# Linear attention one sequence per step instead of in pairs, and an LSTM scratch tile in PSUM

## The chip, the cores and the metric

The kernel is one program on one core of a Trainium2 chip. The metric is device time in microseconds (us) of one execution. TensorE (PE) does matmuls and transposes, VectorE (DVE), ScalarE (ACT) and GpSimd (POOL) do elementwise work, SyncE issues DMAs. Each has its own in-order queue; they meet through semaphores only.

## The reference, cut to what matters

Twelve layers run over 16 sequences of 128 tokens by 128 features. Each computes `x = layernorm(x + layer(x))`. The change touches two of them.

The first is an LSTM of 20 units over 128 tokens, whose states steer a Gaussian attention:

```python
g = xg_t + h @ W_hh.T
i, f, gg, o = jnp.split(g, 4, axis=-1)
c = jax.nn.sigmoid(f) * c + jax.nn.sigmoid(i) * jnp.tanh(gg)
h = jax.nn.sigmoid(o) * jnp.tanh(c)
```

The fourth is causal linear attention with 16 heads of 8 features, and a layernorm of its own:

```python
q = (jax.nn.elu(q) + 1.0 + FEAT_EPS) / jnp.sqrt(jnp.asarray(E, q.dtype))
k = jax.nn.elu(k) + 1.0 + FEAT_EPS
kv_cumsum = jnp.cumsum(jnp.einsum('blhe,blhf->blhef', k, v), axis=1)
num = jnp.einsum('blhe,blhef->blhf', q, kv_cumsum)
den = jnp.einsum('blhe,blhe->blh', q, jnp.cumsum(k, axis=1))[..., None] + FEAT_EPS
out = (num / den).reshape(B, L, D) @ Wout.T + bout
return (out - mu) / jnp.sqrt(var + LN_EPS) * gamma + beta
```

Both kernels compute it as scores k q^T, kept where the key is not later than the query and zero elsewhere, times V with a column of ones that yields the denominator.

## The kernel before, in words

All 16 sequences stay in SBUF (`x_all`); each stage (S_LSTM, S_X0, S_SIM, S_REG, S_LIN, S_X1, ...) reads and overwrites them. Each engine runs its own function of a stage, then the next stage's; `seq_done` counts finished sequences. Nothing is planned: the order is written out by hand, per engine.

The linear-attention stage, S_LIN, uses the general `att_*` functions with `kind == "linear"`. They work on pairs: sequence s of a pair (s = 0 or 1) has `arena[s]` and the four PSUM banks `ps[s]`. A hardware loop goes over seven of the eight pairs. For each pair:

- POOL copies x (line 471), widens the queries to four head slots (`widen`, line 451), and takes reciprocal square roots as powers (`rstd`, line 356).
- PE does the scores: four matmuls of 32 rows (four heads) by 512 columns in four banks (line 550); values, 16 matmuls of 32 output rows (line 572); four transposes (line 600); projections of the pair two further on (lines 525 to 538); the transpose of the head output (609) and the output projection (616, bias 338).
- DVE multiplies each 128x512 bank of scores by a triangle of zeros and ones (line 746), divides by the denominator (772 to 783), makes the feature map from Exp (714, 732 to 736), and does both layernorms (798, 362 to 379, 811, 371).
- ACT only copies out of PSUM (639, 655, 682, 690) and takes one Exp (660).

What precedes S_LIN is S_REG, of the same functions; what follows is S_X1 (lines 1809 on). S_FF1 (lines 1920 to 2042) and S_FF2 are written in another manner: a Python loop, fully unrolled, of one sequence per step, in which each engine works in one step on several sequences in different phases.

The LSTM is 128 steps, each a ring of PE (line 1504), ACT (1530, 1533), DVE (1547, 1549), ACT (1535, which writes the tanh of the cell, `tanh_c`, a tile of 20x16 in SBUF), DVE (1552, which reads it and writes the state). Bank `ps[0][0]` holds in this time only the means of four weight matrices, once, in step 25.

## Time and profile before

| | us |
|---|---|
| median of 3 runs (2166.25 to 2170.86) | 2168.05 |
| the profiled execution | 2166.34 |
| its span, first to last instruction | 2164.5 |
| busy in the span: PE | 1637.6 |
| DVE | 1280.6 |
| ACT | 917.1 |
| POOL | 539.3 |

The mean granted clock of PE was 0.847 of full speed. A line of the profile names the source line, engine and operation, then output and input tiles, and how often it came; busy time and mean duration follow, then the time for which the engine was idle just before, with what ended it. PE matmuls are pipelined: a matmul in fp32 is recorded as two instructions.

### The profile page before, as it was taken

To read this page: it belongs to the slowest core of one execution; us is meant where nothing else is said; L and a number is where in the kernel's file an instruction comes from. 1 tells how busy PE (TensorE), PEld (TensorE's weight loads), DVE (VectorE), ACT (ScalarE), POOL (GpSimd) and SP (SyncE) were. 2 spreads that over 40 slices of the span, in tenths; PEclk is the share of its full clock that TensorE was granted. 3 is DMA by queue.
4 is the path that set the end of the run, shared out by engine and by line. 5 is a ranking of instruction groups with operands and counts; after the bars stand their busy time and mean duration, and the time that the engine had idled before them with its cause. 6 is when DMAs were issued, how large, how long until landed. Compare 5 with 4: busy or idle time off the path is not lost.

```text
span 2164.5 us, 44201 instructions
## 1 busy us (share of the span) xinstructions
PE 1637.6 (76%) x14699; PEld 1045.7 (48%) x14699; DVE 1280.6 (59%) x3907; ACT 917.1 (42%) x2683; POOL 539.3 (25%) x902
## 2 busy tenths in 40 slices
PE   4555489767776556889777863389799999996997
PEld 3333355434443335545444532156467777773443
DVE  2333556556666775721675768766656666653776
ACT  3332334447651113443443444433355665662433
POOL 2321422211112223310122213312134434341110
PEclk6555599779996778899898985599999999997999
DMA  5000000000000000000002000000000000000000
GB/s 199 1 1 1 1 1 0 0 1 0 0 0 0 0 0 0 1 0 1 1 0 101 0 1 0 0 2 0 0 1 1 0 0 0 0 1 0 0 0 19
DMA packets 2933, 18.34 MB, mean 8 GB/s; under 512 B 1049, under 2 KB 1177, under 8 KB 1561
## 3 DMA queue, kind: packets, MB, share of 16 engines
q1 hardware_dynamic: 2842, 17.17, 2.1%
q8 instruction: 52, 0.85, 0.2%
q14 instruction: 39, 0.32, 0.0%
HBM read 16.06 MB, written 1.05 MB: 8 GB/s over the span
## 4 chain that ended last, share of the span: by engine, by line
PE 57%; issue 17%; DVE 9%; ACT 7%; POOL 4%; DVEq 4%; POOLq 1%; DMA 0%; ACTq 0%; SPq 0%
PE ps L2825 5%; PE ps L916 3%; PE ps L930 3%; PE ps L2390 3%; PE ps L2400 3%; PE ps L2414 3%; PE ps L2369 3%; PE ps L2376 3%; PE ps L985 2%; PE ps L2234 2%; PE ps L1504 2%; PE ps L338 2%; POOL arena L356 2%; PE ps L895 2%; PE ps L550 2%
## 5 line engine op out<-in xcount | busy, mean ns | idle before, releaser
L356 POOL TENSOR_TENSOR arena<-arena,C 128x1 f32<-128x1 f32 (+1 forms) x208 | 118.0, 570 | 640.7 <-DVE arena L367 328.7
L1075 DVE TENSOR_REDUCE arena<-ps 128x4 f32<-128x512 f32 x256 | 164.1, 685 | 89.6 <-PE ps L926 50.4
L2327 POOL TENSOR_TENSOR arena<-arena 128x512 f32<-128x512 f32 x128 | 132.7, 1042 | 233.6 <-DVE arena L2615 233.1
L451 POOL TENSOR_TENSOR arena<-arena,C 128x512 f32<-128x512 f32 x96 | 99.8, 1040 | 363.7 <-ACT arena L652 124.6
L1043 ACT ACTIVATE arena<-ps 128x512 f32<-128x512 f32 x256 | 132.2, 603 | 91.5 <-PE ps L942 91.5
L2825 PE MATMUL ps<-WA,arena 128*128 128x512 f32 x256 | 133.4, 603 | 0.4 <-ACT arena L2849 0.4
L1504 PE MATMUL ps<-hid,WA 128*20 128x16 f32 x1024 | 57.2, 196 | 95.5 <-DVE hid L1552 95.5
L2524 ACT ACTIVATE arena<-ps,arena 128x256 f32<-128x256 f32 x256 | 119.9, 477 | 11.8 <-issue 8.1
L2533 ACT COPY arena<-ps 128x512 f32<-128x512 f32 x128 | 69.1, 589 | 121.5 <-PE ps L2400 121.5
L2607 DVE TENSOR_REDUCE arena<-ps 128x2 f32<-128x512 f32 x128 | 82.5, 686 | 43.9 <-PE ps L2390 42.5
L550 PE MATMUL ps<-arena 32*128 32x512 f32 x256 | 54.4, 907 | 63.2 <-POOL arena L451 63.2
L1504 PEld LDWEIGHTS ps<-hid,WA 128*20 128x20 f32 x1024 | 43.6, 116 | 117.7 <-DVE hid L1552 117.2
L338 PE MATMUL ps<-bias,ones_b 128*128 128x128 bf16 (+1 forms) x336 | 98.8, 294 | 0.0
L930 PE MATMUL ps<-arena 32*128 32x512 f32 x512 | 76.8, 671 | 16.8 <-DVE arena L1075 16.7
L916 PE MATMUL ps<-arena 32*128 32x128 f32 x2048 | 77.1, 288 | 15.1 <-DVE arena L1101 11.2
L2857 ACT ACTIVATE arena<-ps 128x256 f32<-128x256 f32 x128 | 49.0, 383 | 91.7 <-PE ps L338 91.7
L916 PEld LDWEIGHTS ps<-arena 32*128 32x128 f32 x2048 | 66.6, 192 | 31.7 <-issue 19.9
L985 PE MATMUL ps<-arena 128*32 128x128 f32 x2048 | 77.8, 281 | 3.6 <-ACT arena L1043 2.7
L371 DVE TENSOR_SCALAR x_all<-arena 128x128 f32 (+1 forms) x160 | 65.9, 412 | 19.9 <-POOL arena L356 19.4
L1547 DVE SCALAR_TENSOR_TENSOR prod<-gates 20x32 f32<-20x32 f32 x128 | 23.0, 180 | 90.7 <-ACT gates L1530 90.7
L2400 PE MATMUL ps<-C,arena 128*128 128x128 f32 x512 | 70.8, 280 | 3.7 <-POOL arena L2327 3.7
L2390 PE MATMUL ps<-arena 64*128 64x256 f32 x512 | 72.6, 402 | 0.0
(444 smaller groups left out, 4110.5 us busy)
## 6 DMA issues: line engine op xcount, KB each, us to landing
WA<-w_late SPq DMA_DIRECT2D x1, 4228.0 KB, 12.9
WA<-w_early SPq DMA_DIRECT2D x1, 1600.0 KB
R<-rows SPq DMA_DIRECT2D x1, 1282.0 KB, 6.8
WB<-w_rest SPq DMA_DIRECT2D x1, 1152.0 KB, 11.2
xT_all<-x_T SPq DMA_DIRECT2D x1, 1024.0 KB, 6.6
x_all<-x_tok SPq DMA_DIRECT2D x1, 1024.0 KB, 13.7
arena<-mask SPq DMA_DIRECT2D x1, 1024.0 KB
ctxT_all<-ctx_T SPq DMA_DIRECT2D x1, 1024.0 KB
```

What stands on the lines that cost most here:

```text
L338: return nc.tensor.matmul(out_ap, ones_b[:, :], bias3[:, BIAS(name, of, width)], start=False, stop=stop, skip_group_check=True)
L356: nc.gpsimd.tensor_tensor(v_(s, cols, "rstd", 0, n), v_(s, cols, "mv", 1, 2 * n - 1)[:, ::2] if n > 1 else v_(s, cols, "mv", 1, 1), cst("m ...
L916: mm = nc.tensor.matmul(ps[z][t][:, 128 * j:128 * j + 128], v_(z, ATT, "P", WIDE_Q + 128 * j, 128)[rows(t), :], v_(z, ATT, "kT")[rows(t), ...
L930: nc.tensor.matmul(ps[s][t][:, :], v_(s, ATT, "kT")[rows(t), :], v_(s, ATT, "P", WIDE_Q, 512)[rows(t), :], start=True, stop=False, skip_gr ...
L985: mm = nc.tensor.matmul(ps[s][2][PAD * j:PAD * (j + 1), t * 128:(t + 1) * 128], va[:, 4 * t + j, :], v_(s, ATT, "PT", 128 * (4 * t + j), 128),
L1043: nc.scalar.activation(v_(s, ATT, "PT", 512 * t, 512), ps[s][t][:, :], ACT.Exp, scale=SCALE).then_inc(pT_sb, 1)
L1075: red = nc.vector.tensor_reduce(v_(z, ATT, "m", 4 * t, 4), heads(ps[z][t][:, :]), AXX, ALU.max)
L1504: mm = nc.tensor.matmul(bank(k // HALF, gt)[:, k % HALF, :], W_of(*weights("hh", gt)), h, start=False, stop=True, skip_group_check=True)
L2327: nc.gpsimd.tensor_tensor(p, p, v_(z, LAT, "rec", 4 * u + 2 * x, 2).unsqueeze(2).broadcast_to([128, 2, 256]), ALU.mult).then_inc(l_sub, 1)
L2390: mm = nc.tensor.matmul(score_bank(u, x)[:, 256 * j:256 * j + 256], v_(z, LAT, "qT", 128 * (2 * u + j), 128)[rows, :], kT[rows, 2 * u + j, :],
L2400: mm = nc.tensor.transpose(score_bank(u, x)[:, 128 * c:128 * c + 128], P_of(s, u, x)[:, 128 * c:128 * c + 128], ident)
L2825: nc.tensor.matmul(o, v_(s, MOE, "xT"), WA[:, W_LATE("experts", FF * e, FF)], start=True, stop=False, skip_group_check=True)
```

## The change

The S_LIN stage gets functions of its own in place of the `att_*` ones: an unrolled pipeline of single sequences. A sequence has one working area, in the arena that its number's parity picks, and all sequences share eight banks: four for scores (`ps[1]`), one for the projections, one for transposes of x and of the head output, one for the values, one for the turned output and the output projection. The triangle is applied by DVE in bank 0 only. In banks 1, 2 and 3 a bf16 matmul adds -2^100 above the diagonal, and ACT evicts with Relu, which leaves the other (positive) scores as they are. The scale of the queries moves into the denominator's addend; the clamp with its addend goes from DVE to POOL, and beta is added to x beforehand, on POOL. Counters of later stages that share semaphores with the new stage are shifted by LIN_STEPS or BATCH. Semaphores of the new stage are declared, run numbers of later stages renumbered. In the LSTM `tanh_c` becomes a slice of PSUM bank `ps[0][0]`, and the weight means move to `ps[1][1]`.

```diff
+LIN = Columns(("xT", 128), ("e", 256), ("f", 256), ("wide", 512), ("PT", 1024), ("OT", 512), ("O", 128), ("OnT", 128),
+              ("rec", 16), ("xb", 128), ("yg", 128), ("r", 128), ("stats", 12), ("mv", 4), ("rstd", 2))
+LIN_AT = QKV_KEPT + 1344
...
-        tanh_c = sb("tanh_c", [LSTM_H, BATCH])
...
+        tanh_c = ps[0][0][0:LSTM_H, 0:BATCH]
...
-                mm = nc.tensor.matmul(ps[0][0][:, 0:4], ones_f[:, :], small[:, at:at + 4], start=half == 0, stop=half == 1)
+                mm = nc.tensor.matmul(ps[1][1][:, 0:4], ones_f[:, :], small[:, at:at + 4], start=half == 0, stop=half == 1)
...
-                nc.vector.tensor_scalar(mean, ps[0][0][:, 0:4], 1.0 / (DIM * FF), 1e-5, ALU.mult, ALU.max)
+                nc.vector.tensor_scalar(mean, ps[1][1][:, 0:4], 1.0 / (DIM * FF), 1e-5, ALU.mult, ALU.max)
...
-                pool.wait_ge(f_var, f1_count(k))
+                pool.wait_ge(f_var, LIN_STEPS + f1_count(k))
...
+        LIN_STEPS = BATCH + 1
+        ACT_BANKS, DVE_BANKS = (1, 2, 3), (0,)
+        s_bank, qkv_bank, x_bank, oT_bank, o_bank = ps[1], ps[0][3], ps[0][2], ps[0][1], ps[0][0]
+        def lin_(n, name, of=0, width=None):
+            c = LIN(name, of, width)
+            return arena[n % 2][:, LIN_AT + c.start:LIN_AT + c.stop]
+        def lin_PT(t):
+            c = LIN("PT", 512 * (t % 2), 512)
+            return arena[t // 2][:, LIN_AT + c.start:LIN_AT + c.stop]
+        def lin_V(n):
+            return arena[n % 2][:, VAUG].rearrange("p (h d) -> p h d", h=HEADS)
+        def lin_steps():
+            return range(-3, BATCH + 4)
+        def lin_count(k):
+            return k - 1
+        def lin_moments(k):
+            return (0 if seq(k - 2) else 1), (2 if seq(k - 3) else 1)
+        def seq(n):
+            return 0 <= n < BATCH
+        def lin_pool(pool):
+            for k in lin_steps():
+                n = k + 1
+                if seq(n):
+                    pool.wait_ge(lin_f, n + 1)
+                    nc.gpsimd.tensor_tensor(heads(lin_(n, "wide")),
+                                            lin_(n, "f", 0, 128).unsqueeze(1).broadcast_to([128, 4, 128]),
+                                            cst("tilemask").unsqueeze(2).broadcast_to([128, 4, 128]),
+                                            ALU.mult).then_inc(lin_wide, 1)
+                n = k + 2
+                if seq(n):
+                    pool.wait_ge(lin_exp, n + 1)
+                    nc.gpsimd.tensor_scalar(lin_(n, "e"), lin_(n, "e"), 1.0, 1e-4, ALU.min, ALU.add).then_inc(lin_low, 1)
+                a, b = lin_moments(k)
+                if a < b:
+                    pool.wait_ge(f_var, lin_count(k))
+                    nc.gpsimd.tensor_tensor(lin_(k, "rstd", a, b - a), lin_(k, "mv", 2 * a + 1, 2 * (b - a) - 1)[:, ::2],
+                                            cst("minushalf")[:, 0:b - a], ALU.pow).then_inc(f_rstd, 1)
+                n = k - 2
+                if seq(n):
+                    nc.gpsimd.tensor_tensor(lin_(n, "xb"), x_all[:, n, :], R[:, ROWS("lin_b")], ALU.add).then_inc(f_xb, 1)
+        def lin_pe(pe):
+            def rows(t):
+                return slice(32 * t, 32 * t + 32)
+            def scores(n):
+                pe.wait_ge(lin_wide, n + 1)
+                for t in DVE_BANKS + ACT_BANKS:
+                    mm = nc.tensor.matmul(s_bank[t][:, :], lin_(n, "f", 128, 128)[rows(t), :], lin_(n, "wide")[rows(t), :],
+                                          start=True, stop=t in DVE_BANKS, skip_group_check=True)
+                    if t in DVE_BANKS:
+                        mm.then_inc(lin_s, 1)
+                for t in ACT_BANKS:
+                    nc.tensor.matmul(heads(s_bank[t][:, :]), causal_b[:, :],
+                                     ident_b[:, :].unsqueeze(1).broadcast_to([128, 4, 128]), start=False, stop=True,
+                                     skip_group_check=True).then_inc(lin_sm, 1)
+            def turned_o(n):
+                pe.wait_ge(lin_oT_sb, n + 1)
+                if n > 0:
+                    pe.wait_ge(lin_yread, n)
+                for t in range(GROUPS):
+                    mm = nc.tensor.transpose(o_bank[:, 128 * t:128 * t + 128], lin_(n, "OT", 128 * t, 128), ident)
+                mm.then_inc(lin_o, 1)
+            def project(n):
+                pe.wait_ge(lin_xT_sb, n + 1)
+                if n > 0:
+                    pe.wait_ge(lin_f, n)
+                    pe.wait_ge(lin_v, n)
+                xT = lin_(n, "xT")
+                for of in (0, 128):
+                    o = qkv_bank[:, of:of + 128]
+                    nc.tensor.matmul(o, W_of("lin", of, 128), xT, start=True, stop=False, skip_group_check=True)
+                    nc.tensor.matmul(o, bias3[:, BIAS("lin", of, 128)], ones_b[:, :], start=False, stop=True,
+                                     skip_group_check=True)
+                o = qkv_bank[:, 256:384]
+                nc.tensor.matmul(o, xT, W_of("lin", 256, 128), start=True, stop=False, skip_group_check=True)
+                add_bias(o, "lin", 256, 128).then_inc(lin_qkv, 1)
+            def normed_T(n):
+                pe.wait_ge(lin_div, n + 1)
+                nc.tensor.transpose(x_bank[:, 128:256], lin_(n, "O"), ident).then_inc(lin_on, 1)
+            def values(n):
+                pe.wait_ge(lin_v, n + 1)
+                done = 0
+                for t in DVE_BANKS + ACT_BANKS:
+                    if t in DVE_BANKS:
+                        pe.wait_ge(lin_tri, len(DVE_BANKS) * n + DVE_BANKS.index(t) + 1)
+                    else:
+                        pe.wait_ge(lin_relu, len(ACT_BANKS) * n + ACT_BANKS.index(t) + 1)
+                    for j in range(4):
+                        mm = nc.tensor.matmul(oT_bank[PAD * j:PAD * j + PAD, 128 * t:128 * t + 128],
+                                              lin_V(n)[:, 4 * t + j, :], lin_PT(t)[:, 128 * j:128 * j + 128],
+                                              start=True, stop=True, skip_group_check=True)
+                mm.then_inc(lin_oT, 1)
+            def output(n):
+                pe.wait_ge(lin_on_sb, n + 1)
+                nc.tensor.matmul(o_bank[:, 0:128], lin_(n, "OnT"), W_of("lin", 384, 128), start=True, stop=False,
+                                 skip_group_check=True)
+                add_bias(o_bank[:, 0:128], "lin", 384, 128).then_inc(f_y, 1)
+            def turned_x(n):
+                pe.wait_ge(seq_done, ready(S_LIN, n))
+                nc.tensor.transpose(x_bank[:, 0:128], x_all[:, n, :], ident).then_inc(lin_xT, 1)
+            for k in lin_steps():
+                if seq(k):
+                    scores(k)
+                if seq(k - 1):
+                    turned_o(k - 1)
+                if seq(k + 2):
+                    project(k + 2)
+                if seq(k - 1):
+                    normed_T(k - 1)
+                if seq(k):
+                    values(k)
+                if seq(k - 1):
+                    output(k - 1)
+                if seq(k + 3):
+                    turned_x(k + 3)
+        def lin_act(act):
+            for k in lin_steps():
+                n = k + 2
+                if seq(n):
+                    act.wait_ge(lin_xT, n + 1)
+                    nc.scalar.copy(lin_(n, "xT"), x_bank[:, 0:128]).then_inc(lin_xT_sb, 1)
+                if seq(k):
+                    for m, t in enumerate(ACT_BANKS):
+                        act.wait_ge(lin_sm, len(ACT_BANKS) * k + m + 1)
+                        nc.scalar.activation(lin_PT(t), s_bank[t][:, :], ACT.Relu).then_inc(lin_relu, 1)
+                n = k - 1
+                if seq(n):
+                    act.wait_ge(lin_on, n + 1)
+                    nc.scalar.copy(lin_(n, "OnT"), x_bank[:, 128:256]).then_inc(lin_on_sb, 1)
+                n = k + 2
+                if seq(n):
+                    act.wait_ge(lin_qkv, n + 1)
+                    nc.scalar.activation(lin_(n, "e"), qkv_bank[:, 0:256], ACT.Exp).then_inc(lin_exp, 1)
+                if seq(k):
+                    act.wait_ge(lin_oT, k + 1)
+                    nc.scalar.copy(lin_(k, "OT"), oT_bank[:, :]).then_inc(lin_oT_sb, 1)
+                if seq(n):
+                    nc.scalar.copy(lin_V(n)[:, :, 0:HD], qkv_bank[:, 256:384].rearrange("p (h d) -> p h d",
+                                                                                        h=HEADS)).then_inc(lin_v, 1)
+        def lin_dve(dve):
+            o_heads = o_bank[:, :].rearrange("p (h d) -> p h d", d=PAD)
+            for k in lin_steps():
+                n = k + 1
+                if seq(n):
+                    dve.wait_ge(lin_low, n + 1)
+                    dve.wait_ge(lin_v, n + 1)
+                    nc.vector.scalar_tensor_tensor(lin_(n, "f"), qkv_bank[:, 0:256], 0.0, lin_(n, "e"), ALU.max,
+                                                   ALU.add).then_inc(lin_f, 1)
+                y, r, done = k - 2, k - 3, k - 4
+                if seq(y):
+                    dve.wait_ge(f_y, y + 1)
+                    nc.vector.bn_stats(lin_(k, "stats", 0, 6), o_bank[:, 0:128])
+                    dve.drain()
+                    nc.vector.bn_aggr(lin_(k, "mv", 0, 2), lin_(k, "stats", 0, 6))
+                    dve.drain()
+                    nc.vector.scalar_tensor_tensor(lin_(y, "yg"), o_bank[:, 0:128], lin_(k, "mv", 0, 1), R[:, ROWS("lin_g")],
+                                                   ALU.subtract, ALU.mult).then_inc(lin_yread, 1)
+                if seq(k):
+                    for m, t in enumerate(DVE_BANKS):
+                        dve.wait_ge(lin_s, len(DVE_BANKS) * k + m + 1)
+                        nc.vector.tensor_tensor(heads(lin_PT(t)), heads(s_bank[t][:, :]),
+                                                cst("triT").unsqueeze(1).broadcast_to([128, 4, 128]),
+                                                ALU.mult).then_inc(lin_tri, 1)
+                if seq(r) or seq(done):
+                    dve.wait_ge(f_rstd, lin_count(k - 1))
+                if seq(r):
+                    dve.wait_ge(f_xb, r + 1)
+                    nc.vector.scalar_tensor_tensor(lin_(r, "r"), lin_(r, "yg"), lin_(k - 1, "rstd", 0, 1), lin_(r, "xb"),
+                                                   ALU.mult, ALU.add)
+                o = k - 1
+                if seq(o):
+                    dve.wait_ge(lin_o, o + 1)
+                    nc.vector.tensor_scalar(lin_(o, "rec"), o_heads[:, :, HD:HD + 1].rearrange("p h d -> p (h d)"),
+                                            1e-4 / SCALE, None, ALU.add)
+                dve.drain()
+                if seq(r):
+                    nc.vector.bn_stats(lin_(k, "stats", 6, 6), lin_(r, "r"))
+                if seq(o):
+                    nc.vector.reciprocal(lin_(o, "rec"), lin_(o, "rec"))
+                if seq(done):
+                    nc.vector.tensor_scalar(x_all[:, done, :], lin_(done, "r"), lin_(k - 1, "mv", 2, 1),
+                                            lin_(k - 1, "rstd", 1, 1), ALU.subtract, ALU.mult).then_inc(seq_done, 1)
+                dve.drain()
+                if seq(o):
+                    nc.vector.tensor_tensor(lin_(o, "O").rearrange("p (h d) -> p h d", d=HD), o_heads[:, :, 0:HD],
+                                            lin_(o, "rec").unsqueeze(2).broadcast_to([128, HEADS, HD]),
+                                            ALU.mult).then_inc(lin_div, 1)
+                if seq(r):
+                    nc.vector.bn_aggr(lin_(k, "mv", 2, 2), lin_(k, "stats", 6, 6))
+                    dve.drain()
+                a, b = lin_moments(k)
+                if a < b:
+                    v = lin_(k, "mv", 2 * a + 1, 2 * (b - a) - 1)[:, ::2]
+                    nc.vector.tensor_scalar(v, v, LN_EPS, None, ALU.add).then_inc(f_var, 1)
...
-                att_pool(pool, S_LIN, "linear")
+                lin_pool(pool)
...
-                att_pe(pe, S_LIN, "linear", WA, "lin", "lin", None)
+                lin_pe(pe)
...
-                att_act(act, S_LIN, "linear")
+                lin_act(act)
...
-                att_dve(dve, S_LIN, "linear")
+                lin_dve(dve)
```

## Rows read from the trace of the kernel before

**Rows 1.** The page: chain shares by engine; POOL's costliest group.

```profile
PE 57%; issue 17%; DVE 9%; ACT 7%; POOL 4%; DVEq 4%; POOLq 1%; DMA 0%; ACTq 0%; SPq 0%
L356 POOL TENSOR_TENSOR arena<-arena,C 128x1 f32<-128x1 f32 (+1 forms) x208 | 118.0, 570 | 640.7 <-DVE arena L367 328.7
```

**Rows 2.** Stretches: us, busy (count) of PE, PEld, DVE, ACT, POOL; clock; DMA.

```profile
643.90:818.90 175.00, 97.80 (x932) 61.49 (x931) 121.81 (x361) 24.25 (x80) 40.84 (x68) 0.72 0.00 0
895.00:925.00 30.00, 27.54 (x162) 17.93 (x161) 25.42 (x100) 16.41 (x31) 13.05 (x21) 1.00 0.00 1
```

**Rows 3.** Waits, 675.2 to 801.5: total us, times, longest.

```profile
PE ps L550 <- POOL arena L451: 48.8, 12, 4.3
```

**Rows 4.** Timeline, one pair: start, us, engine, line, operation, [idle before].

```profile
703.50 0.44 PE L510 MATMUL ps<-C,arena 128*128 128x128 f32 x2
...
706.72 0.39 PE L609 MATMUL ps<-C,arena 128*128 128x128 f32 x2
...
719.08 4.86 DVE L746 TENSOR_TENSOR arena<-ps,C 128x512 f32<-128x512 f32 x8
719.13 2.17 PE L550 MATMUL ps<-arena 32*128 32x512 f32 x8 [4.09 <-POOL arena L451]
...
725.27 0.17 DVE L772 TENSOR_SCALAR arena<-ps 128x16 f32<-128x16 f32 x1 [1.33 <-PE ps L600]
...
725.85 0.29 DVE L783 TENSOR_TENSOR arena<-ps,arena 128x128 f32<-128x128 f32 x1
...
732.62 1.04 POOL L451 TENSOR_TENSOR arena<-arena,C 128x512 f32<-128x512 f32 x1 [0.30 <-DVEq L737]
...
739.98 2.17 PE L550 MATMUL ps<-arena 32*128 32x512 f32 x8 [4.10 <-POOL arena L451]
```

**Rows 5.** Timeline, both ends of the stage.

```profile
643.96 0.22 PE L338 MATMUL ps<-bias,ones_b 128*128 128x128 bf16 x1
...
654.45 3.53 PE L550 MATMUL ps<-arena 32*128 32x512 f32 x16 [2.71 <-POOL arena L451]
...
804.62 3.64 PE L572 MATMUL ps<-arena 128*32 128x128 f32 x64
...
818.87 0.48 PE L1828 MATMUL ps<-C,arena 128*128 128x128 f32 x1 [6.73 <-POOLq L1811]
```

**Rows 6.** Groups by shape, 646.8 to 818.8: busy us, mean ns, idle before.

```profile
L746 DVE TENSOR_TENSOR arena<-ps,C 128x512 f32<-128x512 f32 x64 | 38.9, 675 | 1.1 <-PE ps L550 1.1
L362 DVE BATCH_NORM_STATS2 arena<-arena 128x6 f32<-128x128 f32 x32 | 9.4, 294 | 2.6 <-issue 0.3
L682 ACT COPY arena<-ps 128x512 f32<-128x512 f32 x16 | 9.4, 585 | 119.6 <-PE ps L572 119.6
L732 DVE SCALAR_TENSOR_TENSOR arena<-ps,arena 128x256 f32<-128x256 f32 x16 | 6.8, 424 | 2.3 <-issue 1.4 <-ACT arena L660 0.8
L655 ACT COPY arena<-ps 128x128 f32<-128x128 f32 x16 | 4.2, 265 | 18.0 <-PE ps L338 18.0
```

**Rows 7.** Groups, 0 to 470, S_X0: scores, mask, values.

```profile
L930 PE MATMUL ps<-arena 32*128 32x512 f32 x128 | 19.2, 670 | 2.0 <-DVE arena L1075 1.9
L985 PE MATMUL ps<-arena 128*32 128x128 f32 x512 | 17.9, 276 | 0.9 <-ACT arena L1043 0.7
L936 PE MATMUL ps<-ident_b,m_mask 128*128 128x512 bf16 x64 | 17.1, 391 | 0.0
```

**Rows 8.** Groups of the whole span: ACT's LSTM tanhs, DVE's PSUM and SBUF reads.

```profile
L1535 ACT ACTIVATE tanh_c<-gates 20x16 f32<-20x16 f32 x128 | 27.5, 215 | 54.2 <-DVE gates L1549 54.2
L1533 ACT ACTIVATE gates<-ps 20x16 f32<-20x16 f32 x128 | 20.2, 158 | 0.0
L376 DVE SCALAR_TENSOR_TENSOR arena<-arena,R 128x128 f32<-128x128 f32 x16 | 5.6, 351 | 1.4 <-issue 1.4
L1911 DVE SCALAR_TENSOR_TENSOR arena<-ps,arena,x_all 128x128 f32<-128x128 f32 x16 | 5.6, 351 | 13.4 <-PE ps L1858 11.4 <-issue 2.0
```

**Rows 9.** Activation table loads at S_FF1's Gelu.

```profile
L1997 ACT ACT_TABLE_LOAD x1 | 1.3, 1283 | 0.0
```

More of the change, by code:

```diff
@@ L261, in decoder @@
         reg_add = sem("reg_add")
-        lin_min = sem("lin_min")
+        lin_xT = sem("lin_xT")
+        lin_xT_sb = sem("lin_xT_sb")
+        lin_qkv = sem("lin_qkv")
         lin_exp = sem("lin_exp")
+        lin_v = sem("lin_v")
+        lin_low = sem("lin_low")
+        lin_f = sem("lin_f")
+        lin_wide = sem("lin_wide")
+        lin_s = sem("lin_s")
+        lin_sm = sem("lin_sm")
+        lin_relu = sem("lin_relu")
+        lin_tri = sem("lin_tri")
+        lin_oT = sem("lin_oT")
+        lin_oT_sb = sem("lin_oT_sb")
+        lin_o = sem("lin_o")
+        lin_div = sem("lin_div")
+        lin_on = sem("lin_on")
+        lin_on_sb = sem("lin_on_sb")
+        lin_yread = sem("lin_yread")
         h_sb = sem("h_sb")
@@ L1970, in down @@
                 if n + 2 >= BATCH:
-                    pe.wait_ge(f_var, f1_count(n - 1))
+                    pe.wait_ge(f_var, LIN_STEPS + f1_count(n - 1))
                 y = ps[n % 2][3][:, 0:128]
@@ L2015, in ff1_dve @@
                 if k > -F1_X:
-                    dve.wait_ge(f_rstd, f1_count(was))
+                    dve.wait_ge(f_rstd, LIN_STEPS + f1_count(was))
                 n = k + F1_XN
@@ L2022, in ff1_dve @@
                 if 0 <= n < BATCH:
-                    dve.wait_ge(f_y, n + 1)
-                    dve.wait_ge(f_xb, n + 1)
+                    dve.wait_ge(f_y, BATCH + n + 1)
+                    dve.wait_ge(f_xb, BATCH + n + 1)
                     nc.vector.scalar_tensor_tensor(f1_(n, "r"), ps[n % 2][3][:, 0:128], f1_(was, "rstd", 1, 1),
@@ L2068, in ff2_pool @@
                     taken = 1 if k < 0 else 2 if k < F2_R else 3
-                    pool.wait_ge(f_var, F1_STEPS + f2_count(k))
+                    pool.wait_ge(f_var, LIN_STEPS + F1_STEPS + f2_count(k))
                     nc.gpsimd.tensor_tensor(f2_(k, "rstd", 0, taken), f2_(k, "mv", 1, 2 * taken - 1)[:, ::2],
@@ L2114, in ff2_act @@
                 if has(n):
-                    act.wait_ge(f_var, F1_STEPS + f2_count(n))
+                    act.wait_ge(f_var, LIN_STEPS + F1_STEPS + f2_count(n))
                     nc.scalar.activation(f2_(n, "n"), f2_(n, "u"), ACT.Identity, scale=-1.0,
@@ L2155, in ff2_dve @@
                 if k > -F2_X:
-                    dve.wait_ge(f_rstd, F1_STEPS + f2_count(was))
+                    dve.wait_ge(f_rstd, LIN_STEPS + F1_STEPS + f2_count(was))
                 if has(h):
@@ L2174, in ff2_dve @@
                 if has(r):
-                    dve.wait_ge(f_y, BATCH + r + 1)
-                    dve.wait_ge(f_xb, BATCH + r + 1)
+                    dve.wait_ge(f_y, 2 * BATCH + r + 1)
+                    dve.wait_ge(f_xb, 2 * BATCH + r + 1)
                     nc.vector.scalar_tensor_tensor(f2_(r, "r"), ps[1][2][:, 128 * (r % 2):128 * (r % 2) + 128],
```

21 lines of the change are left out of this document (11 added, 10 removed).

## The prediction, on record before the change was run

> **What bounds the kernel now.** I read the page first, for the chain: TensorE (PE) holds 57% of it, no DMA, so stages are settled by PE or by waits on it [rows 1]. Then the busy time by stretch. The linear-attention stage (S_LIN), which the change rewrites, runs from 643.9 to 818.9 us: 175.0 us, PE busy 97.8, VectorE (DVE) 121.8, ScalarE (ACT) 24.3, GpSimd (POOL) 40.8, and a granted PE clock of 0.72 of full speed, so it alternates between the levels of 2.4 and 1.2 GHz [rows 2]. No engine is full. The waits say why: over six pairs, 126 us, PE waits 48.8 us for the queries that POOL widens behind DVE's passes [rows 3]. The timeline of one pair shows lockstep: scores at 719.13 (behind the second widening), eight maskings on DVE until 723.94, the first division done at 726.14, the next widening only at 732.62, the next pair's same scores at 739.98. A pair takes 20.85 us, a sequence 10.43 [rows 4]. The stage is bound by the dependences of a pair done nearly end to end, DVE carrying most of them.
>
> **The rewritten stage, part by part.** Each step k of the new code does scores and values of sequence k, the turning, division and output of k-1, the projection of k+2, the norms of k-2 and k-3.
>
> PE's work per sequence, at full clock. Scores are the same four 32-row matmuls of 512 columns; the cross-attention stage, which does the same, needs 19.2 us for 16 sequences: 1.2. New are three bf16 mask matmuls of 128x512; the same stage's took 17.1 us for 64: 0.27 each, 0.8 in all, and I take 0.7 since that stage was not all at full clock. Values: 17.9 us for 16: 1.1 [rows 7]. The rest (turned input and output, projection, head output turned, output) is unchanged; for a pair most of it lies in one dense stretch, 703.50 to 707.11, so 1.8 a sequence, and about 0.3 for the output: 2.1 [rows 4]. Sum 5.1.
>
> DVE's work falls: one masking of 0.61 (eight in 4.86) to 0.675 instead of four (three become Relu on ACT), and min, two scalings and the copy of y go. What is left is one combine of 0.42, two statistics of 0.29 with an aggregate of at most that, four passes of about 0.35, the masking 0.65, addend and reciprocal 0.5, division 0.3: about 4.6 with some 0.08 between dependent ones (0.87 from the addend's start to the division's end) [rows 4, 6, 8]. ACT gets three Relu of 128x512 from PSUM. No Relu stands in this trace; the nearest rows are the copy of that shape, 0.585, and at the far end the masking on DVE, 0.675. I take 0.59: ACT 3 x 0.59 + 0.59 + three small copies of 0.27 + an Exp of 256 columns, 0.4, = 3.6 [rows 6]. POOL: widening 1.04, a power 0.57, the clamp of 256 columns and the bias addition, each below the widening, say 0.5: 2.6 [rows 1, 4]. So at full clock nothing is full and a loop through several engines sets the period.
>
> I walk that loop from T, the end of values k-1 on PE. ACT copies it out and then copies V of k+1: T+0.9. DVE combines k+1 (waits for V): 1.37; queued behind it are statistics, aggregate and centering of y k-2 (0.37 + 0.26 + 0.44): 2.5; masking of bank 0: 3.15, r of k-3: 3.5. PE meanwhile does output, turned input, scores and masks (T+0.45 to 2.4), the turning (to 3.0), the projection (to 4.0), so DVE's next wait, for the turned output, is already over. Addend, statistics, reciprocal, normalised x, division, each with its gap: the pair's rows give 0.87 from the addend to the end of division, and the two inserted operations add 0.7: T+5.1 [rows 4, 6]. PE waits for it, turns (0.15), and does values k, whose Relus ended at T+3.7: 6.3. Who is queued behind PE's wait for the division: values k, output, the next scores. So 6.3 us per sequence at full clock, with PE busy 81% of it. At half clock PE's 5.1 becomes up to 10.2; the rows behind the 5.1 hold some stretches at half already, and scores at their slowest took 2.17, below twice 1.2 [rows 4], so I take 9.5, PE-bound.
>
> Which clock? The stage had 0.72 with PE busy 0.56 of it; the feed-forward stage that is already one sequence per step is 1.00 over 30 us with PE busy 0.92 [rows 2]. A PE busy 81% at full clock and nearly always at half is nearer the latter. I take nine tenths of the sequences at full: 0.9 x 6.3 + 0.1 x 9.5 = 6.6. Before 10.43. Bounds: 5.9 (division path 0.4 shorter) to 9.5.
>
> Start and end. Before, the stage behind S_REG had its first scores at 654.45 [rows 5], because POOL staged x only behind its last power. Now PE turns x of sequence 0 right behind its last matmul (644.2): copy, projection, Exp, clamp, combine, widening (0.6 + 1.2 + 0.7 + 0.6 + 0.5 + 1.1) give first scores at 648.9; with DVE and POOL still ending S_REG, 649.2. Sixteen periods: 105.6. The first scores lie 0.45 behind T, so values 15 end at 649.2 - 0.45 + 105.6 = 754.4. From the end of the last values to the next stage's first matmul it took 808.26 to 818.87, 10.6 us [rows 5]; one sequence instead of two, but with the statistics spread over steps 17 to 19 behind two powers: 9.5. Next stage at 763.9 instead of 818.9: **55.0 us less**. If start and end gave nothing the sum is 6 us worse. The counts raised by LIN_STEPS and BATCH move no work; cost nothing. No DMA moves.
>
> **The LSTM's tangent.** tanh_c goes from SBUF to PSUM, once in each of 128 steps, on the path: ACT 0.215, then DVE. No row has ACT writing PSUM. The nearest: ACT's 20x16 tanh reading PSUM took 0.158 against 0.215 reading SBUF, 57 ns; reading is not writing, so I bound it at plus or minus 57 ns, 7.3 us either way. DVE's read costs nothing by the rows: 351 ns with a PSUM operand, 351 without [rows 8]. I take 30 ns less: **3.8 us less**. Moving the weight means to bank ps[1][1] is free: nothing else is in that bank before the fold, 70 steps later.
> The Trainium skill bears on this in two sentences that pull apart. "ScalarE: Activation LUTs" (Step-by-step: what each stage is for) says PSUM is the lower-latency destination for ScalarE, which no row here shows. "Perfetto Trace Analysis" (Optimizing Scalar/DVE Operations) gives about 60 ns of access for DVE on SBUF and 125 on PSUM, 93 and 51 for ScalarE; both at once would make each step 23 ns longer, the sum 2.9 us worse instead of 3.8 better. The two 351 ns rows speak against the DVE half of it.
>
> **The sum.** Profiled execution 2166.3 (span 2164.5 plus 1.8) - 55.0 - 3.8 = 2107.5. The median of the runs shown is 1.7 higher: **2109**.
>
> **Rivals.** (a) The clock stays as it is. Partial matmuls (32 rows, 32 columns) remain, and 0.72 was granted over them. Then 0.44 of the sequences at full: 0.44 x 6.3 + 0.56 x 9.5 = 8.1, 24 us more: 2133. Against it: the dense feed-forward stretch. 0.20.
> (b) The loop through DVE is longer than walked: a hop more for each of its waits, or POOL's widening in the way of a DVE pass. Period 7.5: 14 us more, 2123. For it: the walk gives no slack to DVE's last operations. 0.10.
> (c) Relu and Exp evict each other's activation tables: two loads of 1.283 a sequence on ACT [rows 9], one hidden while ACT waits for masks, the other ahead of Exp, pushing the copy behind values by some 0.9: period 7.5, 2123. Against it: the feed-forward stage alternates Gelu, Identity and copies for 16 sequences with one load [rows 9]. 0.03.
> The Trainium skill, "ScalarE: Activation LUTs" (Table sets: the hidden batching unit), says relu is in every set; by it the loads cost nothing.
> (d) The other side: PE at half clock all through the stage, its 10.2 us of work never overlapped perfectly, waits of 0.4: 10.6 a sequence. The masks are 1.4 of it, bought to relieve a DVE that would then not matter. The next stage starts at 649.2 - 0.45 + 9.5 + 16 P = 658.3 + 16 P; with the LSTM's 3.8 that decides from P = 10.3, and at 10.6 the kernel is 5 us slower: 2173. For it: the old stage stood at half over half its time [rows 2]. Against: PE would be always busy, as in no stretch that stayed low. 0.04.
> (e) The LSTM step loses instead of gaining: 7 us to 11 us worse than forecast, 2118; within the range. 0.08. The forecast itself: 0.55.
>
> **How the numbers follow.** The likeliest is the forecast, 2109, in itself 2098 to 2118 (periods 6.1 to 7.1). The range must reach (a) and (b): 2094 to 2136. Within 0.2% of before (4.3 us, about what a measurement of this kernel can tell) needs a period of 10.0 to 10.5: 0.02. Slower: (d), and a mishap of start or contention: 0.05. Faster: 0.93.
>
> **What would show it.** The stage's steady period, between first scores of neighbouring sequences: 6.3 to 6.6. Its granted clock over 0.9 and PE busy over 0.8. DVE idle about a quarter. Relu of 128x512 near 0.59 and no table loads between. PE waiting on the division once per sequence and on little else. First scores near 649, next stage's first matmul near 764. LSTM step 1.54 instead of 1.57. A period above 8, or a clock near 0.7, makes it wrong.

## The result, and the profile after

The changed kernel takes 2096.99 us (median of 4 runs, 2095.26 to 2098.12) against 2168.7 us (4 runs): a ratio of 0.967, 95% interval 0.9655 to 0.9684, 71.7 us less by the medians. The forecast was 2109, range 2094 to 2136.

Three lines of the page of the kernel after (span; busy time and instructions of each engine; granted clock in 40 slices):

```profile
span 2094.2 us, 43699 instructions
...
PE 1625.0 (78%) x14747; PEld 1037.0 (50%) x14747; DVE 1215.8 (58%) x3764; ACT 938.6 (45%) x2731; POOL 552.0 (26%) x903
...
PEclk9999999869999988998989955699899999997999
```

The span is 70.3 us shorter. The view by stretches of the kernel after (us, busy time of PE, PEld, DVE, ACT, POOL, granted clock, DMA), answering to [rows 2], are the LSTM, the whole linear stage, its steady part, and the longest stretch of it at full clock:

```profile
12.00:209.70 197.70, 106.93 (x1541) 72.97 (x1538) 67.48 (x401) 59.88 (x400) 49.69 (x101) 1.00 0.11 39
...
637.00:747.20 110.20, 90.77 (x984) 56.04 (x984) 57.76 (x221) 49.59 (x130) 53.55 (x69) 0.91 0.01 1
...
660.00:728.00 68.00, 62.91 (x726) 38.44 (x724) 39.29 (x154) 36.50 (x95) 38.41 (x48) 1.00 0.01 2
...
649.90:738.60 88.70, 79.50 (x937) 48.89 (x936) 49.13 (x189) 45.79 (x118) 44.89 (x56) 1.00 0.01 2
```

In the steady part PE is busy 92.5% of the time at full clock; before, 56% at 0.72 [rows 2]. DVE's busy time in the stage fell from 121.8 to 57.8 us; ACT's rose from 24.3 to 49.6 (the stretch of the kernel after takes in 1.6 us before S_REG's last output). The ends of the stage, in the timeline of the kernel after (start us, us, engine, line, operation, output<-input; releaser of the idle time), answer to [rows 5]: S_REG's last output, the first widening and the projection that PE does meanwhile, the first and the last scores, the last values, the last two powers, and the next stage's first matmul.

```profile
638.64 0.22 PE L358 MATMUL ps<-bias,ones_b 128*128 128x128 bf16 x1
...
643.40 1.04 POOL L2263 TENSOR_TENSOR arena<-arena,C 128x512 f32<-128x512 f32 x1 [0.55 <-DVE arena L2395]
643.41 0.77 PE L2312 MATMUL ps<-arena,WA 128*128 128x128 f32 x2 [1.95 <-DVE arena L2395]
...
645.71 2.09 PE L2287 MATMUL ps<-arena 32*128 32x512 f32 x8
...
730.42 1.14 PE L2287 MATMUL ps<-arena 32*128 32x512 f32 x8
...
734.35 1.08 PE L2332 MATMUL ps<-arena 128*32 128x128 f32 x32
...
743.27 0.70 POOL L2274 TENSOR_TENSOR arena<-arena,C 128x2 f32<-128x2 f32 x1 [2.74 <-DVE arena L2442]
...
746.05 0.56 POOL L2274 TENSOR_TENSOR arena<-arena,C 128x1 f32<-128x1 f32 x1 [1.66 <-DVE arena L2442]
...
747.19 0.48 PE L1849 MATMUL ps<-C,arena 128*128 128x128 f32 x1 [6.42 <-POOLq L1832]
```

From the end of S_REG's matmuls to S_X1's first: 108.3 us, before 174.7, so 66.4 less. S_REG's last output itself comes 5.3 us earlier (638.64 against 643.96), nearly all of it the LSTM's gain. Together that is 71.7 at the start of the next stage; the span is 70.3 shorter, so 1.4 us are lost again behind the stage. From first to last scores are 15 periods: 84.7 / 15 = 5.65 us a sequence, 10.43 before [rows 4]. The timeline of one steady period of the kernel after:

```profile
705.78 0.33 PE L2321 MATMUL ps<-C,arena 128*128 128x128 f32 x1 [0.40 <-DVE arena L2433]
...
706.04 1.08 PE L2332 MATMUL ps<-arena 128*32 128x128 f32 x32
...
706.78 1.07 POOL L2270 TENSOR_SCALAR arena<-arena 128x256 f32<-128x256 f32 x1 [2.41 <-ACT arena L2380]
...
707.18 0.59 ACT L2383 COPY arena<-ps 128x512 f32<-128x512 f32 x1 [0.49 <-PE ps L2332]
...
707.67 0.27 ACT L2385 COPY arena<-ps 128x128 f32<-128x128 f32 x1
...
708.05 0.43 DVE L2395 SCALAR_TENSOR_TENSOR arena<-ps,arena 128x256 f32<-128x256 f32 x1 [1.99 <-ACT arena L2385]
...
709.01 0.35 DVE L2404 SCALAR_TENSOR_TENSOR arena<-ps,arena,R 128x128 f32<-128x128 f32 x1
...
709.14 1.58 ACT L2372 ACTIVATE arena<-ps 128x512 f32<-128x512 f32 x3 [1.03 <-PE ps L2292]
709.27 0.68 DVE L2409 TENSOR_TENSOR arena<-ps,C 128x512 f32<-128x512 f32 x1
...
709.48 0.42 PEld L2301 LDWEIGHTS ps<-C,arena 128*128 128x128 f32 x4 [0.44 <-issue]
709.51 0.63 PE L2301 MATMUL ps<-C,arena 128*128 128x128 f32 x4
...
710.17 0.18 DVE L2421 TENSOR_SCALAR arena<-ps 128x16 f32<-128x16 f32 x1
...
711.13 0.29 DVE L2433 TENSOR_TENSOR arena<-ps,arena 128x128 f32<-128x128 f32 x1
...
711.74 1.08 PE L2332 MATMUL ps<-arena 128*32 128x128 f32 x32
```

Values (L2332) repeat after 5.70 us. PE stands still 0.40 us, waiting for the division (L2433). Counted from the end of values, 707.12, DVE's combine (L2395) starts at +0.93, its centering (L2404) ends at +2.24, the denominator (L2421) starts at +3.05, the division ends at +4.30, the next values end at +5.70. The denominator starts 0.03 behind the end of the turned output on PE (L2301, 710.14), and in the midst of DVE's unbroken chain: both arrive together. The turned output writes the bank that the centering reads, so it has to wait for it; its weight loads (PEld) start 0.12 behind the centering's end.

In the view that groups instructions by source line (count, shortest/median/longest ns, first and last start), ACT's last tanh, which answers to L1535 in [rows 8], takes 177 ns instead of 215 in the LSTM after:

```profile
L1556 ACT ACTIVATE ps<-gates x128: 176/177/177, 13.2 to 209.6; 20x16 f32<-20x16 f32 x128
```

From its first to its last start are 127 steps: 196.4 / 127 = 1.546 us each; before, 13.4 to 214.8 gave 1.586, which over 128 steps is 5.0 us.

### The profile page after: what moved, and what is told of

It reads as the page before. It is cut to its first block, busy times and chain, and to the rows that moved or that the text cites. A ratio compares the mean times of both kernels' runs of the same rounds, so it can differ in the third digit from the quotient of the medians.

```text
span 2094.2 us, 43699 instructions
## 1 busy us (share of the span) xinstructions
PE 1625.0 (78%) x14747; PEld 1037.0 (50%) x14747; DVE 1215.8 (58%) x3764; ACT 938.6 (45%) x2731; POOL 552.0 (26%) x903
## 4 chain that ended last, share of the span: by engine, by line
PE 58%; issue 16%; DVE 10%; ACT 7%; DVEq 4%; POOL 3%; POOLq 1%; DMA 0%; ACTq 0%; SPq 0%
PE ps L3061 5%; PE ps L936 4%; PE ps L950 3%; PE ps L2626 3%; PE ps L2636 3%; PE ps L2650 3%; PE ps L2605 3%; PE ps L2612 3%; PE ps L1005 2%; PE ps L2470 2%; PE ps L1525 2%; PE ps L358 2%; PE ps L915 2%; PE ps L1013 2%; PE ps L2597 1%
## 5 line engine op out<-in xcount | busy, mean ns | idle before, releaser
L376 POOL TENSOR_TENSOR arena<-arena,C 128x1 f32<-128x1 f32 (+1 forms) x176 | 99.5, 568 | 532.6 <-DVE arena L1131 303.3
L471 POOL TENSOR_TENSOR arena<-arena,C 128x512 f32<-128x512 f32 x80 | 83.2, 1041 | 357.5 <-ACT arena L672 128.2
L2760 ACT ACTIVATE arena<-ps,arena 128x256 f32<-128x256 f32 x256 | 120.1, 478 | 11.8 <-issue 8.1
L950 PE MATMUL ps<-arena 32*128 32x512 f32 x512 | 75.8, 663 | 16.8 <-DVE arena L1095 16.7
L2650 PE MATMUL ps<-arena 128*64 128x128 f32 x1024 | 70.0, 279 | 2.3 <-ACT arena L2769 2.3
L3061 PEld LDWEIGHTS ps<-WA,arena 128*128 128x128 f32 x256 | 48.8, 193 | 44.4 <-issue 29.6
```

The lines of the kernel that those rows point to most:

```text
L950: nc.tensor.matmul(ps[s][t][:, :], v_(s, ATT, "kT")[rows(t), :], v_(s, ATT, "P", WIDE_Q, 512)[rows(t), :], start=True, stop=False, skip_gr ...
L2650: mm = nc.tensor.matmul(half_bank(u)[XD * x:XD * x + XD, at:at + 128], V[:, k, 4 * u + 2 * j + x, 0:XD], PT_of(s, u, x)[:, 256 * j + 128 * ...
L2760: nc.scalar.activation(P_of(z, u, x)[:, 256 * j:256 * j + 256], score_bank(u, x)[:, 256 * j:256 * j + 256], ACT.Exp, scale=-1.0, bias=v_(z ...
L3061: nc.tensor.matmul(o, v_(s, MOE, "xT"), WA[:, W_LATE("experts", FF * e, FF)], start=True, stop=False, skip_group_check=True)
```

## The experiments

Each ratio is against the kernel before on the same chip. The kernel after was also run once more, beside both and on the chip of cell_psum, o_first and order_all:

> The changed kernel again, on the same chip as the run beside it: 2097 within 2.

Measured: 2097.5 us, 0.9683 (0.967 to 0.9696), the same as in the first comparison.

**The tangent alone** (`tangent_only`): the kernel before with

```diff
-        tanh_c = sb("tanh_c", [LSTM_H, BATCH])
...
+        tanh_c = ps[0][0][0:LSTM_H, 0:BATCH]
```

and with the weight means moved to `ps[1][1]`, as in the change.

> The kernel before with one part of the change: tanh_c in PSUM bank ps[0][0], weight means in ps[1][1]; S_LIN as before. In the trace after, ACT's tanh of the cell took 177 ns instead of 215 and the LSTM's 128 steps 1.55 us each instead of 1.59. Theory: the 39 ns of a step are all of this part's gain and it adds to the rest: 5.0 us less, about 2163.7. Rival: the LSTM gained because the changed kernel's profiled run had TensorE at the full clock there (1.00 against 0.51 before), so this kernel at 0.51 gains nothing (2168.7).

Measured: 2161.7 us against 2167.6, ratio 0.9979 (0.997 to 0.9988): 5.9 us less by the medians, 4.6 by the ratio, 2.6 to 6.5 by its interval. In its profiled execution the LSTM ran at the lower clock, as in the trace of before. The stretch of the LSTM in this kernel:

```profile
12.00:209.70 197.70, 106.67 (x1540) 72.83 (x1538) 67.69 (x401) 59.78 (x400) 49.87 (x101) 0.51 0.11 38
```

and from its timeline the last tanh of one step:

```profile
200.55 0.18 ACT L1535 ACTIVATE ps<-gates 20x16 f32<-20x16 f32 x1 [0.42 <-DVE gates L1549]
```

A step took 1.548 us. The gain is the tangent's, and the clock in the LSTM is worth nothing that shows: the repeated kernel after had 0.52 there, the first one 1.00, and both 1.546 a step.

**All masks on DVE** (`dve_masks`), from the kernel after:

```diff
-        ACT_BANKS, DVE_BANKS = (1, 2, 3), (0,)
+        ACT_BANKS, DVE_BANKS = (), (0, 1, 2, 3)
```

> The changed kernel with all four score banks masked on DVE, no mask matmuls, no Relu. Theory: the pipeline of single sequences is most of the gain, and a sequence's period (5.70 us after) is set by DVE's part of the loop at least as much as by PE's; three more maskings of 0.61 us lengthen it to 7.5: 16 x 1.8 = 29 us more, about 2126. Rival 1: PE bounds the stage (busy 62.9 of 68.0 us), so taking 0.8 us of mask matmuls from each sequence pays for DVE's load: 2097 or less. Rival 2: the split of the masking, not the pipeline, made the gain: period near the old 10.4, 2165 or more.

Measured: 2136.9 us, 0.9859 (0.9844 to 0.9874): 31 us less than before, 40 more than after. Of the 31, about 5 are the LSTM's. So the pipeline, with DVE still masking everything and no Relu at all, gives about 26 of the stage's 66 us, two fifths (the clamp and the addition of beta on POOL are part of it), and the split of the masks the rest. Both rivals fall, and so does the theory's "most of the gain". The 40 are more than the 29 expected. The timeline of dve_masks, DVE's combines alone (one per sequence):

```profile
690.76 0.42 DVE L2395 SCALAR_TENSOR_TENSOR arena<-ps,arena 128x256 f32<-128x256 f32 x1 [1.99 <-ACT arena L2385]
...
698.20 0.43 DVE L2395 SCALAR_TENSOR_TENSOR arena<-ps,arena 128x256 f32<-128x256 f32 x1 [2.00 <-ACT arena L2385]
...
707.58 0.43 DVE L2395 SCALAR_TENSOR_TENSOR arena<-ps,arena 128x256 f32<-128x256 f32 x1 [2.99 <-ACT arena L2385]
```

The first of these periods is 7.44 us, near the expected 7.5, at a granted clock of 0.93; the second is 9.38, at 0.69. The values that end in each, on PE:

```profile
696.19 1.08 PE L2332 MATMUL ps<-arena 128*32 128x128 f32 x32
...
704.72 1.94 PE L2332 MATMUL ps<-arena 128*32 128x128 f32 x32
```

The scores ahead of them took 1.14 and 2.09. Both lie on the loop, and their 1.81 us more are nearly all of the 1.94 us between the two periods. From the fourth to the last combine the mean period is 8.34. That asked for the next one.

**Needless PE work** (`dve_masks_twice`): as dve_masks, with three mask matmuls a sequence put back.

```diff
-                for t in ACT_BANKS:
+                for t in (1, 2, 3):
                     nc.tensor.matmul(heads(s_bank[t][:, :]), causal_b[:, :],
                                      ident_b[:, :].unsqueeze(1).broadcast_to([128, 4, 128]), start=False, stop=True,
-                                     skip_group_check=True).then_inc(lin_sm, 1)
+                                     skip_group_check=True).then_inc(lin_s, 1)
```

> The kernel with all four banks masked on DVE (2136.9 us), with the three mask matmuls per sequence put back although DVE masks anyway: 0.8 us of needless PE work a sequence. In that kernel a period took 7.45 at full PE clock, but 8.2 to 9.4 where the clock fell, and its mean was 8.3 with a granted clock of 0.82. Theory: the granted clock follows PE's busy share; more PE work raises it, the DVE-bound period comes nearer to 7.45, and the kernel gets faster by 5 to 12 us, about 2128. Rival: the added work only adds: same or up to 13 us slower.

Measured: 2130.3 us, 0.9828 (0.9813 to 0.9843): 6.5 us less than without this work. The same stretch by the view of stretches, of dve_masks and then of this kernel:

```profile
660.00:745.00 85.00, 58.94 (x593) 38.52 (x591) 53.57 (x164) 15.46 (x50) 32.13 (x40) 0.84 0.01 1
```

```profile
660.00:745.00 85.00, 63.56 (x671) 38.80 (x671) 55.22 (x171) 16.28 (x55) 33.84 (x43) 0.92 0.01 1
```

PE is busier and its clock higher, 0.92 instead of 0.84, and the DVE-bound stage got faster: from the fourth to the last combine its mean period is 7.81 instead of 8.34. The intervals of the two ratios (up to 0.9843, and from 0.9844) only just part; clock and period are the second sign of it. It doesn't follow that the mask matmuls of the kernel after earn their time by the clock: without them (`no_mask_mm`, below) it had 1.00 in the steady part too.

**All masks on ACT** (`act_masks`), from the kernel after:

```diff
-        ACT_BANKS, DVE_BANKS = (1, 2, 3), (0,)
+        ACT_BANKS, DVE_BANKS = (0, 1, 2, 3), ()
```

> The changed kernel with all four score banks masked by matmul and evicted by Relu on ACT, nothing masked on DVE. Theory: two paths reach DVE's denominator together, one through DVE (its r pass ends at 704.52), one through PE (turned output ends at 704.44); freeing DVE of 0.68 us leaves the PE path, now with a fourth mask matmul of 0.27: period 5.9, 3 to 4 us more, about 2101. Rival: DVE's path alone decides: 0.6 less per sequence, 10 us less, 2087.

Measured: 2098.1 us, 0.9679 (0.9664 to 0.9693): the same as after. The expected loss of 3 to 4 us did not come, nor the rival's gain of 10. The period is 5.74. PE's turned output ends 0.05 later behind the combine than in the kernel after, and DVE, freed of its masking, arrives no earlier. The timeline of act_masks:

```profile
703.33 1.04 POOL L2263 TENSOR_TENSOR arena<-arena,C 128x512 f32<-128x512 f32 x1
...
703.57 0.95 DVE L2416 SCALAR_TENSOR_TENSOR arena<-arena 128x128 f32<-128x128 f32 x1
...
703.89 0.60 PE L2301 MATMUL ps<-C,arena 128*128 128x128 f32 x4
...
704.52 0.18 DVE L2421 TENSOR_SCALAR arena<-ps 128x16 f32<-128x16 f32 x1
```

The r pass (L2416), 0.35 in the kernel after, where it starts 0.20 before the widening's end, takes 0.95 here, where nearly the whole widening runs beside it, and ends 0.15 behind it. The denominator starts 0.03 behind the turned output (704.49), as in the kernel after, and where the r pass ends. So this run doesn't tell which of the two held it.

**No mask matmuls** (`no_mask_mm`): the 48 are left out, banks 1 to 3 unmasked.

> The changed kernel without its 48 mask matmuls; banks 1 to 3 are left unmasked, so keys later than the query count there. Theory: PE's path to the turned output gets 0.8 us shorter, but DVE's path (combine, statistics, centering, masking, r) reaches the denominator no earlier than before, so the period stays within 0.1 of 5.70 and the time within 2 us of 2097. Rival (PE is the bound, busy 92% of the stage): the period falls by most of 0.8, 11 us less, 2086.

Measured: 2096.1 us, 0.9673 (0.9658 to 0.9688), the same as after, with PE busy 53.5 us instead of 62.9 in the steady 68. PE now waits before the turned output for DVE's centering (L2399 here), and DVE arrives where it did. The steady part and the timeline of no_mask_mm:

```profile
660.00:728.00 68.00, 53.53 (x686) 35.55 (x678) 39.70 (x155) 36.23 (x94) 38.82 (x49) 1.00 0.01 2
...
701.84 0.35 DVE L2399 SCALAR_TENSOR_TENSOR arena<-ps,arena,R 128x128 f32<-128x128 f32 x1
...
702.34 0.63 PE L2296 MATMUL ps<-C,arena 128*128 128x128 f32 x4 [0.73 <-DVE arena L2399]
...
703.01 0.18 DVE L2416 TENSOR_SCALAR arena<-ps 128x16 f32<-128x16 f32 x1
```

PE at 92% was not the bound. The weight loads of the turned output start at 702.31, 0.12 behind the centering's end, the same 0.12 as in the kernel after. So it was most likely the centering, on DVE, that released the turned output there too, and not the masks in front of it in PE's queue; the profile of the kernel after, which names no releaser, doesn't show it outright.

**Another order** (`o_first`, `order_all`). In both, DVE does the centering before the combine, and the division right behind the masking, ahead of `r` and the norms. In order_all PE also turns the output before the mask matmuls, which is this part of its edit:

```diff
                 if seq(k):
                     scores(k)
                 if seq(k - 1):
                     turned_o(k - 1)
+                if seq(k):
+                    masks()
```

> The changed kernel with another order on DVE only: centering of y k-2 ahead of the combine of k+1, and the division of k-1 right behind the masking, ahead of r of k-3, the normalised x of k-4 and their statistics. Theory (two paths, DVE's and PE's, reach the denominator together; behind it lies work that needs not be there): division ends 0.4 us earlier, then PE's own order binds; period 5.70 to about 5.35, 5 to 6 us less, 2091. Rival: the loop closes through POOL (Exp, clamp 1.07, power, bias, widening, r pass, which in three kernels ended 0.15 us behind the widening), and stays at 5.70: 2097.

> As o_first, and PE turns the output of k-1 before the three mask matmuls instead of behind them. Theory: both paths are now shortened, PE has no wait left and is the bound at its own work of 5.2 us: 8 us less than the changed kernel, 2089. Rival: the Relus start later and values wait for them, no better than o_first.

Measured: o_first 2088.0 us, 0.9636 (0.9623 to 0.9649); order_all 2087.2 us, 0.963 (0.9617 to 0.9643). Both beat the kernel after by more than their intervals; the loop through POOL, which o_first's rival proposed, falls. Between themselves the times can't tell them apart; values repeat after 5.15 (700.52, 705.67) and 4.98 (700.16, 705.14). The timeline of o_first, from one sequence's values to the next, and its steady stretch:

```profile
700.52 1.08 PE L2332 MATMUL ps<-arena 128*32 128x128 f32 x32
...
704.49 0.17 DVE L2414 TENSOR_SCALAR arena<-ps 128x16 f32<-128x16 f32 x1 [0.47 <-PE ps L2301]
...
705.07 0.29 DVE L2419 TENSOR_TENSOR arena<-ps,arena 128x128 f32<-128x128 f32 x1
...
705.41 0.33 PE L2321 MATMUL ps<-C,arena 128*128 128x128 f32 x1
...
705.67 1.08 PE L2332 MATMUL ps<-arena 128*32 128x128 f32 x32
```

```profile
660.00:725.00 65.00, 63.66 (x756) 40.73 (x744) 45.90 (x160) 37.81 (x98) 39.66 (x50) 1.00 0.01 2
```

The same of order_all:

```profile
700.16 1.08 PE L2334 MATMUL ps<-arena 128*32 128x128 f32 x32
...
705.14 1.08 PE L2334 MATMUL ps<-arena 128*32 128x128 f32 x32
```

```profile
660.00:725.00 65.00, 64.15 (x805) 43.19 (x806) 45.95 (x166) 38.35 (x102) 39.61 (x50) 1.00 0.01 2
```

PE is busy 98 to 99% of the stretch: now it is the bound. It was o_first that took the wait away; it gained more than expected (9.5 us against 5 to 6). Where from, its timeline says. Counted again from the end of values (701.60), the denominator starts at +2.89 instead of +3.05: DVE is there 0.47 early and waits for PE, whose turned output no longer waits for a late centering. From the denominator's start to the division's end it takes 0.87 us instead of 1.25, since the statistics and the normalised x no longer stand between. That makes 0.54 of the 0.55 by which the period fell, and more than two thirds of it lie behind the point at which the paths meet.

**The cell in PSUM too** (`cell_psum`):

```diff
-                nc.scalar.activation(tanh_c[:, :], gates[:, 3, :], ACT.Tanh, scale=0.5).then_inc(cell_tanh, 1)
+                nc.scalar.activation(tanh_c[:, :], cell_ps, ACT.Tanh, scale=0.5).then_inc(cell_tanh, 1)
...
+                nc.vector.scalar_tensor_tensor(cell_ps, prod[:, 1, :], 0.5, prod[:, 0, :],
+                                               ALU.mult, ALU.add).then_inc(cell_new, 1)
                 nc.vector.scalar_tensor_tensor(gates[:, 3, :], prod[:, 1, :], 0.5, prod[:, 0, :],
-                                               ALU.mult, ALU.add).then_inc(cell_new, 1)
+                                               ALU.mult, ALU.add)
```

> The changed kernel with the cell state written to PSUM too: DVE writes it first to ps[0][0], from where ACT's last tanh of the step reads it, then to SBUF for the next step, while ACT works. Theory: ACT's read from PSUM is shorter than from SBUF as much as its write is (38 ns; the rows of before show 158 against 215), DVE's write to PSUM costs nothing: 128 steps by 38 ns, 5 us less, 2092. Rival: DVE's write to PSUM is slower than to SBUF or its second pass delays the state: same or slower.

Measured: 2093.8 us, 0.9661 (0.9646 to 0.9676), 3 us below after by the medians, but the intervals overlap. The trace is clearer, in the view by source line of cell_psum:

```profile
L1557 ACT ACTIVATE ps<-ps x128: 146/146/146, 13.1 to 206.6; 20x16 f32<-20x16 f32 x128
...
L1571 DVE SCALAR_TENSOR_TENSOR ps<-prod x128: 170/172/172, 12.9 to 206.4; 20x16 f32<-20x16 f32 x128
```

The tanh takes 146 ns, 31 less; DVE's write to PSUM 172 against 164 to SBUF, 8 more. A step is 1.523, 23 ns less, which is just the difference of the two, 2.9 us in all. The theory's direction holds, at three fifths of its size: ACT gained 31 ns and not 38, and DVE's write to PSUM was not free.

**Both** (`both`): order_all with cell_psum.

> order_all together with cell_psum. Theory: the two add, since one works in the LSTM and one in S_LIN: from order_all's 2087.2 the LSTM's steps take 23 ns less each in cell_psum's trace (1.524 against 1.547), 2.9 us: about 2084, 13 below the changed kernel. Rival: cell_psum's part is no gain beyond noise: 2087.

Measured: 2082.1 us, 0.9616 (0.9603 to 0.9629), beside the kernel after at 2097.5 on the same chip: 15.5 us less by the medians, the fastest of all, and near the 2084 expected.

## Why the prediction was right, and where its sizes were off

The mechanism was right: the pair's lockstep went, a loop through ACT, DVE and PE set the period, PE waited once for the division, the clock came up. The size of its main term was not: the period of 5.65 us lies below the lowest that was held possible, 5.9, and the total of 2097.0 a little below the 2098 to 2118 of the forecast in itself. It is within the range partly by luck. Start and end of the stage came out 4.2 us longer than forecast; had they been as forecast, the total would be about 2093, under the range's 2094. Term by term:

- The stage: 55.0 us forecast, 66.4 measured. Its period is where the difference lies: 6.6 forecast, 5.65 measured, 15 us over the stage, of which start and end took 4 back. Of the 0.95, 0.3 was the share of half clock; from 649.9 to 738.6 the clock was full, so rival (a) and the other side (d) did not come.
- The other 0.6 was my walk of the loop. It was right up to the end of DVE's combine (+1.37 forecast, +1.36 measured), and on PE up to the end of the turned output (+3.0 forecast, +3.02 measured). Behind the combine DVE's chain went faster: centering ended at +2.24 and not +2.5, the denominator started at +3.05 and not about +3.5. From there to the end of the division I added the inserted statistics and normalisation as 0.7 to the pair's 0.87; it took 1.25 and not 1.6. Only the stretch from the division to the end of the values was longer than walked, 1.40 against 1.2. I had added up durations with a gap behind each; the rows overlap where one operation does not need the one before it (the combine is recorded until 708.48, the statistics behind it start at 708.39).
- By the same mistake DVE's work was forecast as 4.6 us a sequence; 39.29 of 68.00 us busy at 5.70 makes 3.3, and DVE was idle 42% of the time, not a quarter. ACT had 3.1 instead of 3.6, POOL 3.2 instead of 2.6.
- PE's work per sequence: 5.1 forecast; 62.91 of 68.00 us busy at 5.70 makes 5.27. The busy time is not all work: in order_all, with the same matmuls, a whole period is 4.98. Relu took 0.599 mean for the 0.59 taken from the copy, with no table load in the stage, so rival (c) is out.
- POOL's clamp of 256 columns was mis-sized: 0.5 forecast as if it went by columns, 1.07 measured. It ends 0.2 before the combine starts, so it cost nothing in the steady part.
- The start: first scores came 6.9 us behind S_REG's last matmul, not 5.0. The first widening ended at 644.44, 0.6 later behind S_REG than those 5.0; the clamp, 1.09 where the sum had 0.6, is one cause, the first projection, 1.9 where it had 1.2, another. The other 1.3 I had not seen at all: PE's queue had the projection of sequence 1 in front of the first scores, from 643.41 to 645.7 (granted clock 0.51 from 642 to 650).
- The end: 9.5 forecast, 11.8 measured from the last values to the next stage. Behind the last output there are two powers on the path, as forecast (743.27 and 746.05); a price for each step was not given, so which part was too low can't be said. The granted clock was 0.53 from 738.0 on.
- The tangent: 3.8 forecast; 39 ns a step, 5.0 us, in the trace, 5.9 by the medians of its own run. The step before was 1.586, not 1.57. On the disputed rule the trace decides: ACT's write to PSUM is 38 ns shorter (215 to 177), and DVE's read from PSUM costs nothing that shows (157 ns with `tanh_c` in PSUM, 164 before), so rival (e) is out. The 30 ns taken were a guess within 57 either way, and came near. The Trainium skill, "ScalarE: Activation LUTs" (Step-by-step: what each stage is for) has ScalarE nearer to PSUM than to SBUF: the trace agrees, with the 38 ns. The Trainium skill, "Perfetto Trace Analysis" (Optimizing Scalar/DVE Operations) has DVE slower on PSUM: these 7 ns don't bear it out for the read; for the write, cell_psum has 8 ns more, not the 65 between its two figures.
- Rival (b), a loop longer than walked: wrong by its sign; the loop was shorter.
- What I did not see: how evenly two paths met at the denominator. "DVE's next wait is already over" was stated with 0.5 us to spare; there was 0.03. That is why fewer matmuls on PE (no_mask_mm) did not move the time; with fewer masks on DVE (act_masks) the r pass grew by 0.60 of the 0.68 that DVE had saved, and both ends came together again. The new order took time off both paths and off what stands behind them.

Left open: how much of the 66.4 us is the clock's. Before, the stage was at half clock over half its time, and dve_masks_twice shows that a higher clock can go with 6 us less where DVE holds the loop; the kernel before with a clock kept up was not tried.

## What to carry to other kernels

When no engine is full, walk the loop of one period operation by operation and look for two paths that meet. Shortening one alone gives nothing. What gives is to move work that isn't needed out of the way, in front of the meeting point on both paths and above all between it and the operation that everyone waits for. In such a walk, count an independent operation put between dependent ones as partly free. Before work is removed from a busy engine, ask whether it waits: at 92% busy, PE was still not the bound. A stage in which PE waits a good deal may run its PE at half clock on top of the wait, so a first gain of overlap can be followed by a second one; how large that was here is open.

## What the runs showed of the hardware

- Work added to PE made a stage faster: 2136.9 to 2130.3 us, granted clock 0.84 to 0.92 in the same stretch. In a kernel with PE busy 79% of its steady part (53.5 of 68 us, no_mask_mm) the clock was 1.00 without such work.
- In the LSTM the same program ran at 1.00 in one execution and 0.52 in another, with 1.546 us a step in both: this ring of small matmuls with ACT and DVE did not gain from the clock.
- ACT's 20x16 tanh: 215 ns from SBUF to SBUF, 177 from SBUF to PSUM, 158 from PSUM to SBUF [rows 8], 146 from PSUM to PSUM. DVE's pass of that size: 164 to SBUF, 172 to PSUM.
- POOL's clamp with addend of 128x256 took 1.07 us, as long as its product of 128x512, 1.04 [rows 4].
- A DVE pass with its operands in SBUF (L2416), 0.35 in the kernel after, took 0.95 in act_masks, started 0.24 behind POOL's widening. The centering (L2404), which reads PSUM, stayed at 0.35 beside the same widening.
